# A four-layer convolution kernel: who forms the remainders of the inner points in the two filtered convolutions

## The reference, cut to what matters

```
m3  = (j - i) % 4 == 0                       # a grid over output and input channels
out = conv3x3(x, w3 * m3)                    # layer 2, x is group-normalised
out = out + einsum('oi,bihw->bohw', w1 * ~m3, x) + b.sum(axis=1)

out = relu(bn1(conv3x3(x, w1)))              # layer 3, x is group-normalised
out = bn2(conv3x3(out, w2))
return relu(out + residual)                  # residual = the layer's own input
```

## Time and profile before

| | |
|---|---|
| median of three runs | 3944.39 us (3941.78 to 3946.97) |
| profiled execution, its time | 3944.6 us |
| its span | 3942.8 us |
| granted TensorE clock, mean | 0.973 of 2.4 GHz |
| masked layer, first part's points to last statistics | 3186 to 3456 us |
| pair, first part's points to the last residual | 3469 to 3940 us |

### The profile page before, as it was taken

One profiled execution on the slowest core, in us unless ns is written; L12 is line 12 of the kernel. 1 busy time (PEld: TensorE's weight loads), 2 busy tenths in 40 slices (PEclk: granted clock), 3 DMA queues, 4 the chain that ended last, 5 costly groups with the idle time before them and its releaser, 6 DMA issues. The chain is left out here.

```text
span 3942.8 us, 107339 instructions
## 1 busy us (share of the span) xinstructions
PE 3611.9 (92%) x30684; PEld 3103.1 (79%) x30684; DVE 2543.2 (65%) x6194; ACT 2168.5 (55%) x5969; POOL 1835.0 (47%) x3002
## 2 busy tenths in 40 slices
PE   7989898989989898969999999999999958879998
PEld 4656566666656565659999999999999957769888
DVE  6868687777868686863333333333333289989998
ACT  5868687777868686854443333333333334345554
POOL 2737474655646364730003333333334457756665
PEclk9999999999999999989999999999999979989999
DMA  4111111111111111111110000000002100000000
GB/s 167 39 56 39 56 39 55 39 51 45 40 56 39 55 39 55 40 61 48 52 54 0 0 0 0 0 0 0 0 28 64 48 10 1 1 13 33 33 33 33
DMA packets 170042, 140.43 MB, mean 36 GB/s; under 512 B 31776, under 2 KB 158368, under 8 KB 166688
## 3 DMA queue, kind: packets, MB, share of 16 engines
q1 hardware_dynamic: 138400, 123.78, 9.5%
q10 hardware_dynamic: 31360, 12.87, 1.2%
HBM read 83.32 MB, written 53.22 MB: 35 GB/s over the span
## 5 line engine op out<-in xcount | busy, mean ns | idle before, releaser
L193 PE MATMUL bank<-h,w_hh 128*128 128x128 f32 x8032 | 933.8, 275 | 0.0
L193 PEld LDWEIGHTS bank<-h,w_hh 128*128 128x128 f32 x8032 | 917.0, 192 | 0.0
L1528 ACT ACTIVATE Pr<-bank,nmx 128x256 f32<-128x256 f32 x1568 | 722.5, 473 | 276.2 <-DVE nmx L1631 270.3
L238 ACT ACTIVATE h<-bank,bg 128x128 f32<-128x128 f32 x1008 | 370.2, 367 | 818.3 <-PE bank L193 818.2
L1465 POOL TENSOR_TENSOR Pr<-Pr,rden 128x512 f32<-128x512 f32 (+1 forms) x784 | 659.6, 855 | 168.1 <-DVE rden L1691 137.9
L1631 DVE TENSOR_REDUCE nmx<-bank 128x1 f32<-128x256 f32 x1568 | 554.5, 416 | 155.1 <-PE bank L1791 153.8
L1455 POOL COPY kg<-kT 128x64 f32 x1568 | 300.1, 238 | 594.8 <-DMA row<-ix 296.0
L284 DVE SCALAR_TENSOR_TENSOR inp<-bank,b_in,tz 128x256 f32<-128x256 f32 x196 | 85.8, 479 | 697.2 <-ACT tz L221 697.2
L1537 ACT ACTIVATE PT<-bank 128x512 f32<-128x512 f32 x784 | 428.8, 610 | 21.1 <-PE bank L1804 21.1
L257 POOL CAST h_hi<-h 128x512 fp32r<-128x512 f32 x196 | 119.9, 612 | 685.1 <-ACT h L238 685.1
L1804 PE MATMUL bank<-ident,Pr 128*128 128x128 f32 x3136 | 436.2, 283 | 0.0
(11 more groups left out here) (261 smaller groups left out, 7310.9 us busy)
## 6 DMA issues: line engine op xcount, KB each, us to landing
vg<-v_windows SPq DMA_DIRECT2D x1176, 32.0 KB, 2.0
first_gates<-gate_sums SPq DMA_DIRECT2D x28, 512.0 KB, 2.6
gate_sums<-first_gates SPq DMA_DIRECT2D x28, 512.0 KB, 3.6
X<-in_x SPq DMA_DIRECT2D x8, 1568.0 KB, 17.8
vg<-v_windows ACTq DMA_DIRECT2D x392, 32.0 KB, 2.3
x_backup<-X SPq DMA_DIRECT2D x8, 1568.0 KB, 5.8
out<-X SPq DMA_DIRECT2D x7, 1568.0 KB, 5.2
v_windows<-vst SPq DMA_DIRECT2D x56, 192.0 KB, 2.1
```

The costliest lines, as they stand in the source:

```text
L193: ins = pe.matmul(bank[m][:, tt * COLS:(tt + 1) * COLS], w_hh[:, k, m * 128:(m + 1) * 128], prev[:, k, :], start=False, stop=(k == NH - 1) ...
L238: act.activation(h[:, 2 * q + tt, m, :], bank[m][:, tt * COLS:(tt + 1) * COLS], ACT.Tanh, bias=bg[:, 0, m:m + 1]).then_inc(s_h, 1)
L1528: act.activation(Pr[:, par, j, :], bank[j][:, 0:KEYS], ACT.Exp, bias=nmx[:, par, j:j + 1], accum_out=den[:, par, j:j + 1])\
```

## The change

In both layers `lo` on GpSimd keeps only half 0, the outer points, and the vector engine gets a function `lo` of its own for half 1, the inner points. The vector engine issues it behind outputs(q), for part q+2, ahead of the part's statistics (masked layer) and of the next last_output. The one semaphore of the remainders becomes two, one for each engine, and TensorE and `points` wait for each where they waited for the one. No arithmetic changes.

```diff
@@ masked_conv, GpSimd; the same in conv_pair @@
                 def lo(q):
-                    for h in range(2):
-                        pool.wait_ge(s_hi, 2 * q + h + 1)
-                        pool.tensor_tensor(halves(v[:, q % 3, 1], h), halves(pts, h),
-                                           halves(v[:, q % 3, 0], h).bitcast(F32), ALU.subtract).then_inc(s_lo, 1)
+                    pool.wait_ge(s_hi, 2 * q + 1)
+                    pool.tensor_tensor(halves(v[:, q % 3, 1], 0), halves(pts, 0),
+                                       halves(v[:, q % 3, 0], 0).bitcast(F32), ALU.subtract).then_inc(s_lo, 1)
...
@@ vector engine, points @@
                     if q:
-                        dve.wait_ge(s_lo, 2 * q - 1)
+                        dve.wait_ge(s_lo, q)
                     dve.tensor_tensor(t[SLOT[0]], d[0], d[2], ALU.subtract)
                     dve.tensor_tensor(t[SLOT[3]], d[1], d[3], ALU.subtract).then_inc(s_pt, 1)
                     if q:
-                        dve.wait_ge(s_lo, 2 * q)
+                        dve.wait_ge(s_lv, q)
                     dve.tensor_tensor(t[SLOT[1]], d[1], d[2], ALU.add)
                     dve.tensor_tensor(t[SLOT[2]], d[2], d[1], ALU.subtract).then_inc(s_pt, 1)
+
+                def lo(q):
+                    dve.wait_ge(s_hi, 2 * q + 2)
+                    dve.tensor_tensor(halves(v[:, q % 3, 1], 1), halves(pts, 1),
+                                      halves(v[:, q % 3, 0], 1).bitcast(F32), ALU.subtract).then_inc(s_lv, 1)
...
                 points(0)
+                lo(0)
                 points(1)
+                lo(1)
                 for q in range(NQ):
...
                     if q + 2 < NQ:
                         points(q + 2)
                     outputs(q)
+                    if q + 2 < NQ:
+                        lo(q + 2)
                     if q >= 2:
                         part_stats(q - 2)
...
@@ tensor @@
-                    pe.wait_ge(s_lo, 2 * q + 2)
+                    pe.wait_ge(s_lo, q + 1)
+                    pe.wait_ge(s_lv, q + 1)
```

More of the change, by code:

```diff
@@ L726, in masked_conv @@
         s_z0, s_z = sem("pad_zero"), sem("conv_z_ready")
-        s_pt, s_hi, s_lo = sem("conv_points_ready"), sem("conv_points_hi_ready"), sem("conv_points_lo_ready")
+        s_pt, s_hi = sem("conv_points_ready"), sem("conv_points_hi_ready")
+        s_lo, s_lv = sem("conv_outer_lo_ready"), sem("conv_inner_lo_ready")
         s_m, s_s1, s_e, s_x = sem("conv_products_ready"), sem("conv_first_product_copied"), sem("conv_outputs_formed"), sem("conv_x_added")
@@ L917, in conv_pair @@
         s_k, s_kr, s_u = sem("pair_bn_steps"), sem("pair_bn_root"), sem("pair_points_split")
[L918 removed]
+        s_z, s_pt, s_hi = sem("z_ready"), sem("points_ready"), sem("points_hi_ready")
+        s_lo, s_lv = sem("outer_lo_ready"), sem("inner_lo_ready")
         s_m, s_s1, s_e = sem("products_ready"), sem("first_product_copied"), sem("outputs_formed")
```

## The result

The changed kernel takes 3954.24 us (median of 15 runs, 3950.76 to 3956.21) where the kernel before, run beside it, takes 3944.53 us (15 runs, 3941.24 to 3946.99). The ratio is 1.0024, with a 95% interval of 1.0016 to 1.0032: slower by 9.7 us, which lies just outside the 0.2% named ahead of it. The profiled execution took 3954.23 us with a span of 3952.4, so its span is 9.6 us longer than that of before (3942.8), and its stretches can be laid against those of before directly.

A forecast was written before the change was run, and what follows sets the result against it. A circle of vector engine, ScalarE and GpSimd was taken to set body lengths, though TensorE is busy for 92%. Pair +0.6 and masked +6 us made +6.6 on 3944.6: 3951 us, likeliest 3943 to 3960, whole range 3927 to 3968.

The forecast's parts named there:

- the likeliest case: Whole kernel: small terms of both signs, 3951 us, own range 3943 to 3960, given 60%.
- The step on which most hung: Both layers: the moved remainder waits about 0.80 us for GpSimd's half, then takes 0.95 us.
- The bodies: Pair: residual bodies 7.68 us, those waiting for mid 6.93, one with neither 5.73, the one after it 7.98.
- the masked body: Masked layer: a body takes 8.34 us against 8.03; twenty-six bodies put at +7.8 us.
- The term that was too small: Every body: GpSimd's remaining remainder taken as 2.10 us, from 4.20 for two.
- its start and tail: Pair: first part starts 1.1 us earlier, the tail gives 0.3 back; pair put at +0.6 us.
- The first five parts: Masked layer's start: shorter waits and bodies 0 and 1 without statistics, put at -3.3 us.
- The last parts: Masked layer's end: TensorE's last part waits for last_output, 0.4 us later.
- A (no wait): Both layers: the new remainder does not wait for GpSimd, 0.68 us less per body, 3886 us; 10%.
- B (1.10 behind the wait): Both layers: after its wait the remainder still takes 1.10 us instead of 0.95, +14, 3966 us; 15%.
- C (another turn in the mid bodies): Pair only: finish and first delay hi in mid bodies, 0.30 us each for 24, +7, 3958 us; 7%.
- D (a wait of the masked layer vanishes by order): Masked layer: GpSimd's order changes, a 0.81 us port wait vanishes in most of 32 bodies, 3930 us; 8%.

The follow-up runs named there:

- the third kernel: Changed kernel with the vector engine's remainder issued right behind last_output(q-1) instead of behind outputs(q), in both layers: 3870.07 us, 0.9816 of before.
- the one with 8 columns: Changed kernel with GpSimd's outer remainder formed for only 8 of its 896 columns, the rest staying zero: 3862.75 us, 0.9801 of before.
- run 90: Not a follow-up run or kernel: the words come from "a circle run 90 times", a count of repetitions, so there is no change or time to give.
- the last one: On top of the third kernel, the vector engine forms both remainder halves in the masked layer, GpSimd keeping add_x alone there: 3878.63 us, 0.9837 of before.
- the masked layer only: The change made in the masked layer alone, the pair's code as before: 3950.66 us, 1.0022 of before.
- ahead of outputs: Changed kernel with the vector engine's remainder one place earlier, between points(q+2) and outputs(q), in both layers: 4094.54 us, 1.0385 of before.
- the fastest kernel: On top of the third kernel, the masked layer's statistics moved right behind the remainder, ahead of the points: 3857.05 us, 0.9784 of before.

## Why the prediction came out

**The time and the mechanism.** 3951 us was predicted and 3954.2 measured, within the likeliest case's own range. The step on which most hung, that the moved remainder waits for GpSimd's half and then takes 0.95, holds: 0.945 to 0.956 after the release in all 96, and 1.08 without a wait when the half is cut to 8 columns. The bodies came out at 7.72, 6.97, 5.76 and 7.91 us (medians) for 7.68, 6.93, 5.73 and 7.98 predicted, the image at 57.74 for 57.54, the masked body at 8.39 for 8.34. TensorE is released by last_output in the masked layer, as said; in the pair too, which the text hadn't named.

**The term that was too small.** Each of those bodies but that of 7.91 is 0.03 to 0.05 us longer than predicted, and one number explains it: GpSimd's remainder was put at 2.10 us, half of the 4.20 of a group of two. Alone it takes 2.14 or 2.15. The two of a group overlap in the records: the second starts 2.10 us after the first. The source view of before gives the single one (ns, min/median/max):

```profile
...
L967 POOL TENSOR_TENSOR v_ring<-points,v_ring x128: 2077/2144/2902, 3471.7 to 3924.8; 128x896 fp32r<-128x896 f32 x128
...
```

Over 96 bodies this is about 4 us, more than the whole difference of 3.2 between forecast and measurement. In the pair it makes eight images 3.0 us longer where 1.4 was said; its start and tail gave 1.5 back, so the pair costs 1.5 (predicted 0.6). In the masked layer the 26 bodies cost 10.2 (predicted 7.8 and 1.1). Two of the prediction's own sums don't come out as written: 26 bodies of 8.34 for 8.03 us make 8.1 and not 7.8, and +1.4 less 1.1 less 0.3 makes nothing for the pair and not 0.6. Together they would change the forecast by 0.3 us.

**The ends of the masked layer.** The first five parts were to give 3.3 us back. The points of part 2 did come the 2.1 us earlier that was worked out, but last_output(0) only 0.6, and up to last_output(2) the gain was 1.6 (3219.42 - 3186.09 before, 3218.25 - 3186.51 after). In three of the first four parts the moved remainder lasts 2.0 to 2.1 us instead of 1.8; in the first two of them no output stands ahead of it that would shorten its wait. The last parts, put at 0.4 us lost, gained 0.9. The two misses, 1.7 us too much gain at the start and 1.3 too little at the end, nearly cancel; that is luck.

**The rivals.** A (no wait) falls with L1083 at 1.80 us. B (1.10 behind the wait) falls with 0.96. C (another turn in the mid bodies) falls with 6.97 and with an image of 57.74, which is the sum of the four kinds of body (3 x 7.72 + 3 x 6.97 + 5.76 + 7.91 = 57.74). D (a wait of the masked layer vanishes by order) didn't occur in the change, where all 32 L840 are blocked. Something near it, a port wait of the masked layer that vanishes for some bodies, did make the third kernel and the one with 8 columns faster than expected; but there the GpSimd instruction didn't come late, it was passed over. The price of the place was in the prediction (remainder ahead of last_output); that a better place would bring 2% was not worked out there.

## What to carry to other kernels

Before work is moved from GpSimd to the vector engine, ask of each vector instruction with two SBUF operands which GpSimd instruction it will meet: in these traces their lengths add, so the move pays only if the wait it brings stands behind what others wait for. Put such an instruction right behind the result that releases TensorE and ScalarE, and put vector instructions that read PSUM or have one operand where GpSimd is busy. Read an operation's length from its single instructions, not from half of a group: 0.04 us in a circle run 90 times was the largest error here.

## What had not been expected

**A waiting GpSimd instruction can be passed over.** Where vector instructions with two SBUF operands stand back to back, a GpSimd tensor_tensor that arrives during the first one gets in behind it or waits for the whole run. With a run of five, in the third kernel, 8 got in and 13 were passed over (2.66 or 4.83 us); with six, in the last one, 8 and 21 (2.61 or 5.83); with four, in the kernel with 8 columns, 16 and 13 (2.19 or 3.83). The same run of four passed over nobody in the change, in the masked layer only and ahead of outputs: 29 of 29 got in, in each of the three. So the length of the run doesn't decide. Nor does the start: in all of these add_x starts 0.15 to 0.19 us behind the first of the run, with the same values in both outcomes.

What goes with the outcome is how long GpSimd was idle just before. In the third kernel all 13 that were passed over had been idle for 0.70 to 0.72 us, and of those that got in only one had. With 8 columns all 13 had been idle for 3.65 or 3.66 us, and of the 16 only two; in the last kernel the 21 had been idle for 1.13 to 1.16 or for 6.00 to 6.02, and none of the others. Since the idle time that goes with being passed over differs from kernel to kernel, this tells of the rhythm of the bodies and not of a cause, which stays open. Where add_x followed an instruction of GpSimd's own without a gap it got in 8 times of 8 in the third kernel. With the one-operand statistics in between it got in 28 times of 28, but 27 of these also followed GpSimd's own remainder without a gap, so what the statistics do by themselves isn't shown. That the vector engine is spared by this, for a net 0.7 us in the ordinary bodies of the third kernel and 1.4 with 8 columns, was measured; whether it could be brought about at will was not tried.

**The shared access is full in the masked layer.** In the fastest kernel it is taken, by the sum given with it, nearly throughout the body of 6.99 us, while TensorE needs 6.36. That it is the bound there is argued from this sum; no run shows it by itself. In the pair TensorE is busy for 340 of 340 us.

```profile
...
3304.81:3311.80 6.99, 6.65 (x38) 6.35 (x37) 6.89 (x13) 3.35 (x5) 4.84 (x3) 1.00 0.01 2
3500.00:3840.00 340.00, 340.00 (x1915) 340.00 (x1913) 327.28 (x532) 204.59 (x237) 113.41 (x53) 1.00 0.08 35
...
```
